# Feed-forward weights in bf16 and activations as two scaled fp16 pieces, placed in the room of x

## What is computed

```python
x = L0_attn_query                                       # (8, 1024, 256)
x = layernorm(x + attn_pyramid(x))                      # 16 heads of 16, 4 levels, up-sampled and summed
lin = lambda x, w, s: einsum('bsi,oi->bso', x, w) * s   # w holds only -1, 0, 1; s is one scale per row
h = silu(lin(x, w1_w, w1_s)) * lin(x, w2_w, w2_s)       # 256 -> 1024
h = gelu(lin(h, h1_w, h1_s))                            # 1024 -> 1024, exact gelu
h = gelu(lin(h, h2_w, h2_s))                            # 1024 -> 1024
x = layernorm(x + lin(h, w3_w, w3_s))                   # 1024 -> 256
```

## Time and profile before

| | us |
|---|---|
| time, median of 3 runs | 4006.61 (4002.73 to 4012.16) |
| the profiled execution | 4005.5, of which the span shown by the trace is 4003.7 |
| PE busy | 3642.2 (91% of the span) |
| ACT busy | 2595.1 (65%) |
| DVE busy | 2552.1 (64%) |
| POOL busy | 1051.4 (26%) |

### The profile page before, as it was taken

How to read it: one execution, slowest core, us unless ns; L and a number is a source line. 1 busy time by engine, 2 the same in 40 slices (tenths; PEclk the granted TensorE clock), 3 DMA queues, 4 the chain that set the end, 5 groups by cost and what they waited for, 6 DMA issues and landing times. The chain is left out here.

```text
span 4003.7 us, 70655 instructions
## 1 busy us (share of the span) xinstructions
PE 3642.2 (91%) x20993; PEld 1954.6 (49%) x20993; DVE 2552.1 (64%) x4806; ACT 2595.1 (65%) x3273; POOL 1051.4 (26%) x1024
## 2 busy tenths in 40 slices
PE   5899889989989989989988988869999999999998
PEld 3333333333333323333333332258878787887887
DVE  5778978878878887887897898523333333333333
ACT  2779778868868868877877978734444344443443
POOL 2233434434444343343443342210000000000000
PEclk6989989989989989998998999979999999999999
DMA  4423423422332332333332344210000000000000
GB/s 138 156 70 98 123 77 91 118 81 86 105 95 87 105 107 79 103 95 93 89 117 72 99 123 135 75 51 12 12 12 13 21 11 12 12 11 13 21 11 11
DMA packets 231920, 284.40 MB, mean 71 GB/s; under 512 B 53524, under 2 KB 189908, under 8 KB 230384
## 3 DMA queue, kind: packets, MB, share of 16 engines
q1 hardware_dynamic: 222272, 270.54, 22.5%
q10 hardware_dynamic: 9216, 8.39, 0.6%
HBM read 166.63 MB, written 108.00 MB: 69 GB/s over the span
## 5 line engine op out<-in xcount | busy, mean ns | idle before, releaser
L982 ACT ACTIVATE a_probs<-a_p_s,a_unit_now 128x1024 f32<-128x1024 f32 x1360 | 1448.7, 1111 | 351.9 <-PE a_p_s L1300 345.3
L1086 DVE TENSOR_REDUCE a_part_max<-a_p_r 128x1 f32<-128x512 f32 x2048 | 1301.6, 676 | 270.9 <-PE a_p_r L1313 266.4
L1313 PE MATMUL a_p_r<-a_k_st,a_q_st 48*128 48x512 f16 (+2 forms) x2944 | 921.0, 383 | 209.5 <-DVE a_part_max L1086 126.2
L1313 PEld LDWEIGHTS a_p_r<-a_k_st,a_q_st 48*128 48x128 f16 x2944 | 229.1, 94 | 1239.6 <-DVE a_part_max L1086 871.3
L1642 PE MATMUL p_h<-f_h_hi,f_w_hi 128*128 128x512 f32 x2048 | 807.3, 394 | 24.0 <-issue 24.0
L1642 PE MATMUL p_h<-f_h_lo,f_w_hi 128*128 128x512 f32 x2048 | 803.2, 392 | 0.0
L1330 PE MATMUL a_p_o<-a_probs,a_v_aug 128*17 128x512 f32 (+2 forms) x5888 | 747.5, 588 | 3.5 <-ACT a_raw L992 2.8
L1300 PE MATMUL a_p_s<-a_q_st,a_k_st 50*128 50x512 f16 (+2 forms) x2944 | 694.9, 376 | 25.9 <-ACT a_probs L982 24.0
L1613 DVE TENSOR_TENSOR f_h_lo<-f_h_f,f_h_hi 128x512 fp32r<-128x512 f32 x256 | 177.1, 692 | 697.2 <-ACT f_h_hi L1539 697.2
L1537 ACT ACTIVATE f_h_f<-p_h,f_sc 128x512 f32<-128x512 f32 x256 | 176.6, 690 | 556.7 <-PE p_h L1642 556.6
L1086 DVE TENSOR_REDUCE a_row_max<-a_p_r 128x1 f32<-128x512 f32 (+2 forms) x672 | 427.2, 676 | 98.2 <-PE a_p_r L1313 95.9
(11 more groups left out here) (131 smaller groups left out, 4533.6 us busy)
## 6 DMA issues: line engine op xcount, KB each, us to landing
qk_scratch<-a_qk_room SPq DMA_DIRECT2D x288, 128.0 KB
a_w_lo<-wqkv_inner SPq DMA_DIRECT2D x30, 768.0 KB, 4.3
a_q_st<-qk_scratch SPq DMA_DIRECT2D x64, 192.0 KB, 3.7
a_k_st<-qk_scratch SPq DMA_DIRECT2D x64, 192.0 KB, 4.8
a_a_lo<-a_attn SPq DMA_DIRECT2D x384, 32.0 KB, 2.0
a_o_lo<-wo_inner SPq DMA_DIRECT2D x24, 512.0 KB, 3.7
a_qk_room<-wf SPq DMA_DIRECT2D x22, 512.0 KB, 3.8
w_lo_scratch<-a_qk_room SPq DMA_DIRECT2D x22, 512.0 KB, 2.7
```

What stands on the lines that cost most here:

```text
L982: act.activation(probs[:, s % 2, 2 * p:2 * p + 2, :], p_s[:, 2 * p:2 * p + 2, :], ACT.Exp, scale=unit_now[:, lvl:lvl + 1]).then_inc(exp_do ...
L1086: dve.reduce_max(out, src, AX.X).then_inc(max_read.sem, 1)
L1313: ins = pe.matmul(p_a[:, r * size:(r + 1) * size], q_st[rows_of(j, ROWS), query_at:query_at + 128], k_st[rows_of(j, ROWS), key_at:key_at + ...
```

## The change

The weights of the first layer and of the two middle layers (20 of the 22 chunks) are held as bf16 instead of fp32r, and their low part, stored for the case that it is needed, as two bf16 pieces. The activations of these layers are held as two fp16 pieces. So that fp16's small range does: x is multiplied by 2^11, and the inputs of the two middle layers by powers of two (`unit`, `up`) that come from a bound worked out on the chip, from the scales and the largest weight of the middle matrices. For that DVE takes the largest absolute value of 12 chunks after they are placed (`ftop`). The last layer's weights and activations stay fp32r; its two chunks are cut in the last sequence straight into their final room and are not stored.

With this the cutting of a chunk becomes longer: POOL subtracts three times (the middle piece, the rest, the low piece), and three chunks are due 7 steps apart. The high parts take half the bytes and find room where x and the projections' weights of attention lie, so that all are placed in five pieces from step 41.5 to step 53.5 of the last sequence, and none at its end. The identity and the scales are loaded once and kept for both parts.

```diff
-PER_BATCH, CHUNKS = 3, 22
-CHUNK_AT, CHUNK_GAP = 3.6, 5.6
-LAST_CHUNK_AT = 27.2
+PER_BATCH = 3
+STORED_CHUNKS = PER_BATCH * (B - 1)
+CHUNK_AT, CHUNK_GAP = 3.6, 7
+W3_AT, W3_GAP = 27.2, 5.6
...
-PLACES = place_order()
+PLACES = [Piece(0, 6, 41.5), Piece(6, 4, 44.5), Piece(10, 4, 47.5), Piece(14, 3, 50.5), Piece(17, 3, 53.5)]
+TOP_AT, TOP_GAP = 58.3, 3
...
+        body += [(at + by, kind, 1, n) for kind, by in (("fload", 0), ("fhi", 1.9), ("fout", 2.8), ("flo", 2.3), ("flow", 4.8), ("fstore", 6.4))]
+        body += [(at + 4.6 + .5 * part, "fcheck", 1, 2 * n + part) for part in range(2)]
...
+    end += [(TOP_AT + TOP_GAP * n, "ftop", 0, n) for n in range(TOPS)]
...
                         elif kind == "flo":
                             pool.wait_ge(f_hi_done.sem, f_hi_done.value(it, n + 1))
-                            pool.tensor_tensor(out=f_raw.bitcast(F32R), in0=f_raw, in1=f_cut, op=ALU.subtract).then_inc(f_lo_done.sem, 1)
+                            if n >= PER_BATCH:
...
+                                pool.tensor_tensor(out=f_w3_lo[:, part], in0=f_raw, in1=f_w3[:, part], op=ALU.subtract).then_inc(f_lo_done.sem, 1)
+                                continue
+                            pool.tensor_tensor(out=f_cut[:, 1, :], in0=f_raw, in1=f_cut[:, 0, :], op=ALU.subtract).then_inc(f_mid_done.sem, 1)
+                            pool.wait_ge(f_mid_done.sem, f_mid_done.value(it, n + 1))
+                            pool.sem_inc(held.sem, 1)
+                            pool.tensor_tensor(out=f_raw, in0=f_raw, in1=f_cut[:, 0, :], op=ALU.subtract).then_inc(f_lo_done.sem, 1)
+                        elif kind == "flow":
...
+                            f_hi_out.wait(pool, it, n + 1)
...
+                            pool.tensor_tensor(out=f_cut[:, 0, :], in0=f_raw, in1=f_cut[:, 1, :], op=ALU.subtract).then_inc(f_low_done.sem, 1)
...
+                        elif kind == "ftop":
+                            dve.wait_ge(f_placed[piece_of(n)].sem, 16)
+                            dve.tensor_reduce(tops[:, n:n + 1], f_hi[:, n * HCOLS:(n + 1) * HCOLS], AX.X, ALU.max, apply_absolute_value=True)
...
-        xt_hi, xt_lo = sb("xt_hi", [128, 2, 512], F32R), sb("xt_lo", [128, 2, 512], F32R)
-        h_hi, h_lo = sb("h_hi", [128, 2, 8, 512], F32R), sb("h_lo", [128, 2, 8, 512], F32R)
+        xt_hi, xt_lo = sb("xt_hi", [128, 2, 512], F16), sb("xt_lo", [128, 2, 512], F16)
+        h_hi, h_lo = sb("h_hi", [128, 2, 8, 512], F16), sb("h_lo", [128, 2, 8, 512], F16)
+        last_hi, last_lo = sb("last_hi", [128, 8, 512], F32R), sb("last_lo", [128, 8, 512], F32R)
...
-                        act.activation(h_hi[:, (half + v // 8) % 2, v % 8, :], h_f[:, v % 2, :], ACT.Copy).then_inc(deep_hi.sem, 1)
+                        if v < 16:
+                            act.activation(h_hi[:, 1, v % 8, :], h_f[:, v % 2, :], ACT.Copy, scale=up[:, 1:2]).then_inc(deep_hi.sem, 1)
+                        else:
+                            act.activation(last_hi[:, v % 8, :], h_f[:, v % 2, :], ACT.Copy).then_inc(deep_hi.sem, 1)
...
+                dve.tensor_reduce(seen[:, 2:3], tops[:, 4:12], AX.X, ALU.max).then_inc(seen_done.sem, 1)
...
+                dve.tensor_scalar(bound[:, 1:2], part[:, 1:2], bound[:, 0:1], FLOOR, ALU.mult, ALU.max).then_inc(bound_done.sem, 1)
...
+                dve.tensor_scalar(up[:, :].bitcast(I32), bound[:, :].bitcast(I32), EXPONENT, EXPONENT, ALU.bitwise_xor, ALU.bitwise_and).then_inc(unit_done.sem, 1)
...
-        w_hi = nc.alloc_sbuf_tensor_at("f_w_hi", [128, FCOLS], F32R, offset=base)
-        w3_lo = nc.alloc_sbuf_tensor_at("f_w3_lo", [128, 8 * E], F32R, offset=base + 4 * FCOLS)
+        w3 = nc.alloc_sbuf_tensor_at("f_w3", [128, 8 * E], F32R, offset=base)
+        w3_lo = nc.alloc_sbuf_tensor_at("f_w3_lo", [128, 8 * E], F32R, offset=base + 32 * E)
+        w_hi = nc.alloc_sbuf_tensor_at("f_w_hi", [128, FCHUNKS * HCOLS], BF16, offset=base + 64 * E)
```

## The result

The changed kernel takes 3955.28 us (median of 4 runs, 3953.94 to 3956.98) where the kernel before takes 4009.39 (4 runs, 4002.73 to 4015.06): a ratio of 0.9866, with an interval of 0.9849 to 0.9883. The profiled execution has a span of 3954.6 us, 49.1 less than that of before. The two executions are compared stage by stage here. The marks are the exponentials on ACT (L982 before, L976 after; 170 per sequence), which read alike in both traces, the load of x for the feed-forward part, and its first matmul.

A forecast was written before the change was run, and what follows sets the result against it. PE's back-to-back matmuls were taken to bound the feed-forward part. 4005.5 - 51.7 (matmuls) + 4 + 1.3 (last sequence) - 3 - 0.9 (seam) = 3955.2, with the runs' median 1.1 higher, so 3956; range 3930 to 3975, also given as 3930 to 3990.

The forecast's parts named there:

- Step 1: First-layer and middle-layer matmuls: 5120 go from 226.8 to 216.7 ns each, a gain of 51.7 us (34.8 to 69.1).
- Step 2: First-layer stretch of the feed-forward part: 120 type changes each way between 16-bit and fp32r matmuls cost 0, at most 24 us.
- B: Feed-forward part: slow type changes cost 24 us and the matmul gain is only 34.8, end 3996; chance with its halves 0.11.
- D: Feed-forward matmuls: bf16 times fp16 keeps the 226.8 ns pitch, so only small terms stay, end 4006.9; chance 0.06.
- Step 3: Feed-forward part: cuts on other engines and the bound's chain of small operations at the start stay hidden: 0, 3.8 if uncovered.
- Step 4: Attention loop: 42 more POOL subtractions, 99.5 us of POOL, eat slack; taken as 0, between -5.6 and +14 us.
- rival C: Attention loop, where chunks are cut: POOL's extra subtractions hold back ACT or DVE, end 4055 at full price; chance 0.07.
- Step 5: Last sequence: five new DVE reductions among the maxima cost +4 us, two more checks +1.3; seven reductions fall in DVE's waits.
- Step 6: Seam from attention to feed-forward: last fetch without placings behind it gains 3 us, x issued 0.9 us earlier.
- the prediction's own sign: End of attention: if the forecast is right, POOL's last residual sum starts within 6 us of its fetch.

The follow-up runs named there:

- the version with late reductions and pairs: Changed kernel with the 12 reductions behind the last maximum and first-layer and last-layer blocks in pairs; 3953.69 us, against 3958.24 for the changed kernel on the same chip.

## Why the prediction was right, step by step

The prediction said 3956 and the time was 3955.3. Its mechanism was right in each main part; that the sum fits to one microsecond is partly luck, since terms that were off leaned against each other. It gives its range once as 3930 to 3975 and once with 3990 as its end; the time lies in both.

- **What bounds the kernel** was right: matmuls back to back in the feed-forward part, and their pitch was the gain. They are not quite back to back: PE stands still for some 5 us five times, before and after alike (last section).
- **Step 1** was taken a little small. The pitch is 215.9 ns, not 216.7, within the bounds (213.3 to 220): 10.9 x 5120 = 56 us instead of 51.7. The sentence on the Trainium skill (page "TensorE: Matmul & The Clock Gate", section "Back-to-back issue gap") had 215.8, and by that rule the trace agrees, though the section gives it for an isolated matmul. The same section also gives some 131 ns for 512 columns in a sustained stream with weight loads; 215.9 in runs of 176 matmuls, each with its weight load, do not bear that out.
- **Step 2** was wrong by its choice of row. It took nothing per change, from bf16 beside fp32r; 36 ns per pair were measured, 4.4 us in all. The other rows had stood for 0.1 us each way, 24 us, so the nearer rows were nearer, but not at zero. The fp32r matmul behind bf16 ones had been read by the start of one record only. Behind that one, at 1185.91, the timeline goes on:

```profile
1186.27 0.41 PE L1190 MATMUL a_p_r<-a_x_hi,a_w_lo 128*128 128x256 f32 x1
1186.48 0.41 PE L1190 MATMUL a_p_r<-a_x_lo,a_w_hi 128*128 128x256 f32 x1
```

  The next one starts 0.36 us after it and the one behind that 0.21 us later, so this row did not show a free change. It gives no price for this one either, with matmuls of 2 columns ahead of it at a granted clock of 0.50. Net of both steps the forecast was -51.7; the measured pitches give 56.0 - 4.4 = 51.6, and the feed-forward part became 50.0 us shorter. Of the rivals, B's 200 ns per pair (0.1 us each way) is out by this, and D's unchanged pitch by step 1.
- **Step 3** was right that the new chain is hidden. It ends at 2645.4, well ahead of the first use of its scales (on ACT, at 2652.66). It left out something small: PE's second matmul of the part starts 1.38 us after the first instead of 0.59, by the timeline of PE, with 0.77 us of "issue" in which the trace shows no wait:

```profile
2648.44 0.61 PE L1678 MATMUL p_h<-f_xt_hi,f_w_hi 128*128 128x512 f16 x1 [1.42 <-DVE f_xt_lo L1594]
2649.82 0.61 PE L1678 MATMUL p_h<-f_xt_lo,f_w_hi 128*128 128x512 f16 x1 [0.77 <-issue]
```

  The granted clock also rises later: it is 0.50 from 2652 to 2654, where it was 1.00 before. So from the first matmul to the first of the middle layers it takes 18.55 us instead of 17.21, though 64 shorter matmuls alone would make it 0.7 less. That is about what the part lacks of 51.6, and it varies: in the eight executions with this feed-forward code it takes 17.2 to 18.6 us.

- **Step 4** was right at 0, within the 10 us by which executions of one loop differ, and rival C was rightly kept at a small chance: its mechanism is real, and the change stays on the near side of it. The size of one subtraction was off, by one line's answer (columns as in the earlier trace rows), which is 2.13 us with bf16 or fp32 results where fp32r took 2.37:

```profile
L900 POOL TENSOR_TENSOR a_qk_room<-a_qk_room x21: 2123/2132/2141, 436.6 to 2394.9; 128x1024 f32<-128x1024 f32 x21
```

  DVE's waits for the subtraction in the loop went, as said, and brought nothing.
- **Step 5** said +5.3, and the last sequence is 5.0 longer. The reductions have +4.1 of the stretch, for +4. One took 1.21 us, not 1.34. The +1.3 for two more checks is not shown by any run: the stretch where they stand (1237th to 1267th exponential) is 1.2 us longer, but two executions of the old code differ by 2.3 us there. That the other seven cost nothing was not quite so: two of them delay a layer norm, 0.9 us.
- **Step 6** was mis-sized: the fetch comes 0.8 us earlier, not 3. This was the low bound (0.8), which came from the earlier fetch with no placing near it; that row was a measurement of the very thing, and leaving it for the middle was the mistake. By the prediction's own sign, POOL within 6 us of the fetch, it was missed too, with 6.25. With the constants and the two late reductions the end of attention is 1.2 us shorter, not 3.9.

So the sum of the terms was -50.3 us and the two spans differ by 49.1, of which 4.7 stand in the opening and the first turn by chance. The medians differ by 54, with a median of before that moved from 4006.61 to 4009.39 when a run was added.

## What to carry to other kernels

A pitch of back-to-back matmuls is a price per instruction that a change of type can lower, and each alternation between types takes some of it back. Putting matmuls of one type together makes the blocks shorter, but here the whole was no shorter for it, so measure the whole. Work on an idle engine is hidden only as long as nobody's small task is queued behind it: look for the shortest slack of what follows it in the queue, not at the busy share, and double it to see how near the edge is. Where a row shows the operation without the disturbance that a change removes, take that row for the gain.

## What the runs showed that was not expected

The work between two marks can be the same and its time not. From the 1237th to the 1267th exponential of the last sequence, the changed kernel and the version with late reductions and pairs did the same instructions (DVE busy 44.31 and 44.41 us), in 54.07 and 58.03 us, in the table of stretches at a mean granted clock of 0.91 and 0.82:

```profile
2404.32:2458.39 54.07, 44.26 (x275) 11.30 (x276) 44.31 (x82) 41.06 (x51) 18.58 (x19) 0.91 0.32 97
```

```profile
2400.44:2458.47 58.03, 48.55 (x275) 12.96 (x276) 44.41 (x82) 41.16 (x50) 18.56 (x19) 0.82 0.29 90
```

The stretches at the lower clock fall differently in each execution, and an attention part of 2640 us differs by several microseconds from one execution to the next. A term of 2 to 4 us has to be read from its own stretch and not from the total, and even that in several executions: this stretch took 53.8 to 58.0 us where nothing of its work was changed.

PE also stands still in the feed-forward part, by the tables of waits (total, times, longest), before and after:

```profile
PE p_h L1642 <- issue: 23.3, 5, 4.9
```

```profile
PE p_h L1678 <- issue: 24.2, 5, 5.1
```

In five of 15 half-passes the first matmul of the middle layers comes some 5 us after the last one of the last layer. In the matmuls behind such a gap the granted clock is 0.50 (table of stretches), and a 16-bit matmul takes 0.43 us there, as an fp32r one did at that clock: the change gains nothing in them.

```profile
2984.35 0.60 PE L1678 MATMUL p_h<-f_h_hi,f_w_hi 128*128 128x512 f16 x1 [4.65 <-issue]
2984.75 0.63 PE L1678 MATMUL p_h<-f_h_lo,f_w_hi 128*128 128x512 f16 x1
2985.18 0.63 PE L1678 MATMUL p_h<-f_h_hi,f_w_hi 128*128 128x512 f16 x1
```

```profile
2984.80:2988.50 3.70, 3.70 (x10) 1.27 (x9) 0.00 (x0) 0.00 (x0) 0.00 (x0) 0.50 0.02 4
```

With the slower matmuls the five gaps come to some 35 us in either kernel, more than any term of the prediction but the first. No trace names their cause, and no run was aimed at them.

Two things more stay open. Why an fp32r matmul takes 226.7 ns and a 16-bit one 215.9 was not taken apart: weight loads became shorter too (1089.0 us for 5874 of them, 618.92 for 5877 after), and no run separates the two. And the 0.77 us of "issue" at the start of the feed-forward part have no cause that the trace names; the runs with the changed start all show it (1.1 to 1.5 us from the first matmul to the second), those with the old one do not (0.59).
